# Four graph layers over 50,000 nodes on one core: the bias of the first product's rows moves from VectorE to TensorE, and ScalarE copies the rows out

## The reference

```python
x = _layernorm(x + _L0_gnn_ref(x, edge_index, ...), axis=-1)      # attention, 4 heads, self loops, gelu, layer norm, + x
x = _layernorm(x + _L1_gnn_ref(x, edge_index, ...), axis=-1)      # three GCN hops
x = _layernorm(x + _L2_gnn_ref(x, edge_index, edge_attr_32, ...), axis=-1)   # attention, 8 heads
x = _layernorm(x + _L3_gnn_ref(x, edge_index, edge_attr_64, ...), axis=-1)   # attention, 4 heads
```

```python
h = x @ W_in + b_in
for i in range(Ws.shape[0]):
    xw = h @ Ws[i]
    msg = xw[src] * norm[:, None]
    agg = jax.ops.segment_sum(msg, dst, num_segments=N) + bs[i]
    h = jax.nn.relu(agg)
```

## Time and profile before

| | us |
|---|---|
| median of 3 runs | 4471.79 |
| the runs | 4471.39 to 4476.36 |
| profiled execution, its own time | 4478.09 |
| its span, first to last instruction | 4476.4 |
| VectorE busy | 3477.6 |
| TensorE busy | 2927.3 |
| POOL busy | 2507.9 |
| ScalarE busy | 2496.4 |

### The profile page before, as it was taken

How to read it: one execution, slowest core, us unless ns; L and a number is a source line. 1 busy time by engine, 2 the same in 40 slices (tenths; PEclk the granted TensorE clock), 3 DMA queues, 4 the chain that set the end, 5 groups by cost and what they waited for, 6 DMA issues and landing times. The chain is left out here.

```text
span 4476.4 us, 48774 instructions
## 1 busy us (share of the span) xinstructions
PE 2927.3 (65%) x12128; PEld 1958.3 (44%) x12128; DVE 3477.6 (78%) x8069; ACT 2496.4 (56%) x5486; POOL 2507.9 (56%) x2300
## 2 busy tenths in 40 slices
PE   5776777777761366665554545558888887577775
PEld 3544445444440133333454544435555555344443
DVE  5999999999997766664665659957777776688886
ACT  3777777777774255553332324445656665455554
POOL 6655655555530376201776767768666661566664
PEclk9889888898885677775877765567777777665665
DMA  5776655555552666651444446622222221333331
GB/s 116 182 186 185 191 181 192 188 182 185 189 170 103 182 182 184 185 177 65 150 152 129 149 144 196 194 74 72 63 70 62 69 63 31 99 84 89 92 92 53
DMA packets 383765, 599.12 MB, mean 134 GB/s; under 512 B 124231, under 2 KB 205296, under 8 KB 383486
## 3 DMA queue, kind: packets, MB, share of 16 engines
q1 hardware_dynamic: 313726, 482.99, 35.1%
q0 software_dynamic: 69760, 113.02, 10.2%
HBM read 312.45 MB, written 287.17 MB: 134 GB/s over the span
## 5 line engine op out<-in xcount | busy, mean ns | idle before, releaser
L1551 POOL DMA_INDIRECT gs_g<-table_xw,slot_idx x588 | 594.2, 1010 | 476.4 <-issue 442.1
L900 POOL DMA_INDIRECT gs_t<-table_x,slot_idx x392 | 418.3, 1067 | 306.1 <-issue 204.4
L495 POOL DMA_INDIRECT gs<-x,src_idx x200 | 224.8, 1124 | 437.3 <-DMA xd_rows<-gd 365.1
L368 PE MATMUL ps<-ident,gs_g 128*128 128x128 f32 x588 | 134.8, 372 | 371.9 <-DMA gs_g<-table_xw,slot_idx 371.9
L1589 ACT ACTIVATE hT_g<-u_g 128x512 f32<-128x512 f32 x147 | 92.5, 629 | 498.3 <-DVE u_g L1638 498.3
L1272 POOL DMA_INDIRECT slot_idx<-node_map,src_idx x200 | 230.5, 1153 | 165.8 <-DMA slot_idx<-node_map,src_idx 69.1
L1631 DVE TENSOR_TENSOR_SCAN agg_g<-same_seg,agg_g,ps 128x512 f32<-128x512 uint8 x147 | 188.0, 1279 | 171.7 <-PE ps L368 171.3
L483 POOL DMA_INDIRECT node_map<-slot_no,end_idx x200 | 280.2, 1401 | 61.0 <-issue 60.0
L1785 POOL DMA_INDIRECT out<-x_t,end_idx x196 | 205.7, 1049 | 169.6 <-ACT x_t L339 116.9
L368 PEld LDWEIGHTS ps<-ident,gs_g 128*128 128x128 f32 x588 | 88.3, 187 | 411.2 <-issue 361.3
L495 POOL DMA_INDIRECT gd<-x,dst_idx x200 | 215.8, 1079 | 60.9 <-issue 60.3
(11 more groups left out here) (362 smaller groups left out, 10069.7 us busy)
## 6 DMA issues: line engine op xcount, KB each, us to landing
table_xw<-xw_b SPq DMA_DIRECT2D x147, 512.0 KB, 4.2
table_x<-x_b SPq DMA_DIRECT2D x98, 512.0 KB, 2.8
own_g<-table_xw SPq DMA_DIRECT2D x147, 256.0 KB, 3.7
x_in<-x SPq DMA_DIRECT2D x49, 512.0 KB
out<-hf_b SPq DMA_DIRECT2D x49, 512.0 KB, 2.8
table_xw<-xw_g SPq DMA_DIRECT2D x98, 256.0 KB, 2.3
pen_t<-pen_row SPq DMA_DIRECT2D x98, 256.0 KB, 4.1
xd_rows<-gd SPq DMA_DIRECT2D x50, 256.0 KB, 5.6
```

What stands on the lines that cost most here:

```text
L368: last = nc.tensor.transpose(to[0:width, j * P:(j + 1) * P], t[:, j * width:(j + 1) * width], ident[:])
L495: pool.indirect_dma_start(out=to[k % 3][:, j * D:(j + 1) * D], out_offset=None, in_=x, in_offset=bass.IndirectOffsetOnAxis(ap=of[:, n:n + ...
L900: pool.indirect_dma_start(out=self.B[L % RING][g][:, t * D:(t + 1) * D], out_offset=None, in_=table, in_offset=bass.IndirectOffsetOnAxis(a ...
L1551: pool.indirect_dma_start(out=gs[c % 6][:, j * D:(j + 1) * D], out_offset=None, in_=tables[layer], in_offset=bass.IndirectOffsetOnAxis(ap= ...
```

## The change

The two additions of `xw0_bias` on DVE (L783) are gone. PE puts the bias into the piece of PSUM first, as a product of a row of ones with `xw0_bias4`, a row that holds the bias four times, and adds the four 128x128 products to it. ACT copies the rows out (`xw0_copy`), one half behind each Relu of `h1T`. ACT's wait for `scaled` moves from ahead of the first Relu to ahead of the applies of `x2`.

```diff
--- before.py
+++ after.py
@@ -416,6 +416,7 @@
         rs, nm = ring("rs", 2, (P, 6, 8)), ring("nm", 2, (P, 6, 8))
         big, half_y, hx, wx = (ring(n, 1, (P, 48))[0] for n in ("big", "half_y", "hx", "wx"))
         shifted = tmp.enter_context(nc.sbuf_tensor("shifted", [P, 48], I32))
+        xw0_bias4 = tmp.enter_context(nc.sbuf_tensor("xw0_bias4", [1, CH], F32))
         LNA, LNB, LNC, LND, LNE, LNF = range(6)
         T_XT, T_H, T_G, T_A, T_B, T_C, T_D = ps[:, 0, :], ps[:, 1, :], (ps[:, 2, :], ps[:, 3, :]), ps[:, 4, :], ps[:, 5, :], ps[:, 6, :], ps[:, 7, :]
 
@@ -529,6 +530,14 @@
                     nc.tensor.matmul(T_H[0:8, :], att_src[:], xsT[k % 2][:], start=True, stop=False)
                     nc.tensor.matmul(T_H[0:8, :], att_dst[:], xdT[k % 2][:], start=False, stop=True).then_inc(S("z_ps"), 1)
 
+                def xw0_rows(to, h):
+                    nc.tensor.matmul(to, ones[:], xw0_bias4[:], start=True, stop=False, skip_group_check=True)
+                    for j in range(SUB):
+                        last = nc.tensor.matmul(to[:, j * D:(j + 1) * D], x1T[h][:, j * P:(j + 1) * P], WI0[:],
+                                                start=False, stop=j == SUB - 1, skip_group_check=True)
+                    last.then_inc(S("xw0_ps"), 1)
+
+                pe.wait_ge(S("xw0_bias4"), 1)
                 for t in range(N_CH + 3):
                     f, m = live(t), live(t - 3)
                     c = t - 3
@@ -547,13 +556,13 @@
                         turn(pe, T_B, half(x1_b[c % 3], 1)).then_inc(S("x1T_ps"), 1)
                         pe.wait_ge(S("x1T"), 2 * c + 1)
                         nc.tensor.matmul(T_C, WI0[:], x1T[0][:], start=True, stop=True).then_inc(S("h1_ps"), 1)
-                        rows_times(pe, T_D, x1T[0], WI0).then_inc(S("xw0_ps"), 1)
+                        xw0_rows(T_D, 0)
                     if f:
                         times_W0(t, 0)
                     if m:
                         pe.wait_ge(S("x1T"), 2 * c + 2)
                         nc.tensor.matmul(T_A, WI0[:], x1T[1][:], start=True, stop=True).then_inc(S("h1_ps"), 1)
-                        rows_times(pe, T_B, x1T[1], WI0).then_inc(S("xw0_ps"), 1)
+                        xw0_rows(T_B, 1)
                     if f:
                         turn_x(t, 1)
                     if m:
@@ -597,6 +606,12 @@
                                                     scale=r[:, n, k:k + 1], bias=b[:, n, k:k + 1])
                     last.then_inc(S(ready), 1)
 
+                def xw0_copy(c, h):
+                    act.wait_ge(S("xw0_ps"), 2 * c + h + 1)
+                    if h == 0 and c >= 2:
+                        landed(act, "xw0_out", 2, c - 2)
+                    nc.scalar.copy(half(xw_b[0][c % 2], h), (T_D, T_B)[h]).then_inc(S("xw0"), 1)
+
                 def copy_xT(c, h):
                     act.wait_ge(S("xT_ps"), 2 * c + h + 1)
                     nc.scalar.copy(xT[h][:], T_XT).then_inc(S("xT"), 1)
@@ -622,17 +637,19 @@
                         nc.scalar.copy(x1T[0][:], T_A).then_inc(S("x1T"), 1)
                         act.wait_ge(S("x1T_ps"), 2 * c + 2)
                         nc.scalar.copy(x1T[1][:], T_B).then_inc(S("x1T"), 1)
-                    act.wait_ge(S("scaled"), t + 1)
                     if m:
                         act.wait_ge(S("h1_ps"), 2 * c + 1)
                         nc.scalar.activation(h1T[0][:], T_C, ACT.Relu, bias=h1_bias[:, 0:1]).then_inc(S("h1T"), 1)
+                        xw0_copy(c, 0)
                     if f:
                         gelu(t, 0)
                     if m:
                         act.wait_ge(S("h1_ps"), 2 * c + 2)
                         nc.scalar.activation(h1T[1][:], T_A, ACT.Relu, bias=h1_bias[:, 0:1]).then_inc(S("h1T"), 1)
+                        xw0_copy(c, 1)
                     if f:
                         copy_xT(t, 1)
+                    act.wait_ge(S("scaled"), t + 1)
                     if live(t - 5):
                         q = t - 5
                         if q >= 3:
@@ -705,6 +722,7 @@
                 def blocks(t):
                     return lambda k: t[:, k * D:(k + 1) * D]
 
+                V.tensor_copy(xw0_bias4.rearrange("o (j f) -> o j f", j=SUB), xw0_bias[0:1, None, :].to_broadcast([1, SUB, D])).then_inc(S("xw0_bias4"), 1)
                 for k in range(2):
                     V.memset(raw[k][:], 1.0).then_inc(S("raw"), 1)
                 v.wait_ge(S("raw"), 2)
@@ -774,13 +792,8 @@
                     v.wait_ge(S("batch"), n0 + 10)
                     V.scalar_tensor_tensor(out=b, in0=of[:, :, 1], scalar=-1.0, in1=r, op0=ALU.mult, op1=ALU.mult).then_inc(S("scaled"), 1)
 
-                    m, c, a = live(t - 3), t - 3, t - 1
+                    a = t - 1
                     for h in range(2):
-                        if m:
-                            v.wait_ge(S("xw0_ps"), 2 * c + h + 1)
-                            if h == 0 and c >= 2:
-                                landed(v, "xw0_out", 2, c - 2)
-                            V.tensor_tensor(rows4(half(xw_b[0][c % 2], h)), rows4((T_D, T_B)[h]), each_row(xw0_bias), ALU.add).then_inc(S("xw0"), 1)
                         if live(a):
                             v.wait_ge(S("scaled"), t + 1)
                             v.wait_ge(S("w"), a + 1)
```

## The result

The changed kernel takes 4491.46 us (median of 6 runs, 4487.80 to 4495.41), the kernel before 4471.43 us in its 6 runs (4467.28 to 4476.36): a ratio of 1.0045, 95% interval 1.0032 to 1.0058. It is 20 us slower. The forecast was 4484, 12 us slower, in a range of 4449 to 4497.

A forecast was written before the change was run, and what follows sets the result against it. DVE bound the node stage; the ACT-PE loop would bind next, 26.27 us at full clock, 27.2 with half clock. 40 iterations at +0.23 (+9) and +3 at the ends make +12 us: 4484, range 4449 to 4497.

The forecast's parts named there:

- signs named: Node-stage profile if the loop binds: `nm` wait below 40 us, ACT waiting for PE, DVE for ACT, clock below 0.9.
- bias matmul: PE's one-row, 512-column matmul, two per iteration on the loop: 1.11 us each, bounds 0.86 and 1.97.
- rival B: Node stage: PE's clock stays up, iterations of 26.3 to 26.45 us; 4451 us, wholly at full clock -25 us; chance 0.22.
- half-clock term: Half clock on the loop's PE work adds 0.78 us to 26.27, making 27.05; with recurring stretches, 27.2 was taken.
- the walk: Half-clock stretches 27.3 us apart meet each 26.97 us iteration 0.3 us later, until the iteration comes near 27.3.
- ends of the stage: Node stage's first iterations: two bias matmuls add 2.2 us to each of two, +4, less 1 for those just behind.
- A: The forecast: the loop through PE and ACT binds with half clock on it, +3 to +20 us; chance 0.50 above +9.
- C: No change: clock on the loop stays 0.93, iteration 26.71 us, or a mild loss; medians 4463 to 4481; chance 0.22.
- D: Bias matmuls are hidden and DVE still binds, needing a loop below 25.6 us: -55 us, 4417; chance 0.02.
- E: Worse: more than +20 us, if ACT's late start also makes DVE wait at the hd rows (L800); chance 0.04.

The follow-up runs named there:

- e1: The changed kernel with the two bias matmuls of each iteration left out: 4417.41 us, ratio 0.9873 to the kernel before.
- e6: The changed kernel with the bias row as three bfloat16 parts over 128 rows, added in one pass: 4415.23 us, ratio 0.9870 to the kernel before.
- e4: The changed kernel with three more unused 128x512 matmuls per iteration on PE ahead of the scores: 4463.03 us, ratio 0.9975 to the kernel before.
- e8: Control: the kernel before with three extra unused 128x512 matmuls per iteration ahead of the scores: 4474.18 us, ratio 1.0001 to the kernel before.
- e7: The changed kernel with each bias matmul issued twice in a row: 4643.30 us, ratio 1.0377 to the kernel before.
- e9: The changed kernel with the fp32 bias matmul on operands of 128 rows instead of one: ratio 0.9908 to the kernel before, on a slower chip.
- e3: The changed kernel with ACT's wait for the batch back ahead of the first Relu: 4567.44 us, ratio 1.0209 to the kernel before.
- e5: The changed kernel with the first half's bias matmul issued earlier, ahead of the scores: 4424.35 us, ratio 0.9884 to the kernel before.
- e12: The same kernel as e9 (changed kernel, bias operands of 128 rows), run once more: ratio 0.9886 to the kernel before, on a slower chip.

## Why the prediction was right, and where its sizes were off

**The direction and the mechanism held.** DVE stopped being the bound, the loop through ACT and PE took over (e1 and e6: without the dear matmuls on it DVE binds again), and half clock on that loop turned a gain into a loss (e4: with a clock of 0.97 the same kernel and more work is 28 us faster; e8: not so in the kernel before). Of the signs named, ACT's wait for `nm` fell to nothing, ACT waits 84.2 / 30 = 2.8 us per iteration ahead of the new copies (3 expected), DVE waits 43.1 / 30 = 1.44 us for ACT's rows (1 to 1.6 expected), and the clock over the first 6 us is 0.80 (below 0.9 expected). One sign failed: the iterations do not alternate between 26.3 and 28.

**The bias matmul was mis-sized.** I took 1.11 us. It is 1.25: 1.05 for itself, and 0.10 each for the product ahead of it (L562, 1.06 instead of 0.96; L568 to the second bias 0.96 instead of 0.86) and the rows behind it (0.99 instead of 0.89). The distances in the earlier trace rows had the 1.05; I compared one neighbour and not both. By e7 and e9 this is better read as 0.86 for the matmul and 0.39 for the change between 128 rows and one. Two matmuls, each 0.14 short, are 0.28 us, and the loop at full clock is 26.57, not 26.27. So rival B could at best have brought (26.57 - 26.97) x 40 + 3 = -13 us, not -25.

**The half-clock term was near, its form was not.** I expected a mixture of iterations of 26.3 and 28 that settles at 27.2. The measured mean is 27.31, but there is no mixture: each iteration loses the same 0.73 us. Nor does a first 6 us at 0.80 cost the 1.2 us that I put on it, since part of it is hidden beside ACT's copies. That 27.05 (26.27 + 0.78) came as near as it did owes something to luck: the 0.78 was the mean of a pattern that did not stay. The argument that the stretches recur 27.3 us apart, and that the walk stops when the iteration reaches that, was the part that held best; its number, 27.3, should have been the forecast instead of the 27.2 between two estimates.

**The ends of the stage.** By the starts of the batches, the 37 steady iterations cost 37 x 0.33 = 12.2 us. The four iterations from 74.0 us take 92.0 us instead of 84.5, +7.5, where I had put +4; the next five +0.5 and the three that follow the steady part +2. Together some +22.6, and the last batch starts 23.0 us later (1453.9 against 1430.9). The +3 I had for both ends was +10. The +7.5 belongs to the bias matmuls: without them (e1) the same four iterations take 83.6 us, and the prediction charged only two of them, for two matmuls of 1.1 each.

**Of the rivals,** A held, and with +20 us at the very end of its +3 to +20. C and B needed a clock of 0.93 and 0.95 or more; it was 0.80. D was excluded by the loop. E's wait at the hd rows did not come (DVE's only waits are those at L821); it did come in e3 (41.6 us), where ACT starts its part late, and in e7 (80.9 us), where the loop was made longer.

**One row or 128.** The Trainium skill, "TensorE: Matmul & The Clock Gate", has a matmul of few rows cost as much as one of 128. Counted alone that agrees with this case: a one-row fp32 matmul behind another adds 0.86 us in e7, and one of 128 rows takes 0.86 in e9. But one that stands between products of 128 rows costs 1.25 in all, and that is the case of this kernel. The Trainium skill's advice in the closing table, to leave PE few idle gaps, is borne out by e4, which that advice would have led to, and brings nothing in e8, where PE is not on the loop. For the changed kernel alone I took it to mean 4451 us, and it measured 4491: the change closes one gap (PE goes from the turn of the next columns at 720.29 straight to the second product at 720.73) but not the one ahead of the scores, 2.30 us.

## What to carry to other kernels

Before work is moved off the engine that binds, write down the loop that will bind next, at full and at half TensorE clock: slack that hides PE also hides its clock (e8), and once the slack is used, what half clock costs shows on the loop (0.73 us per iteration here, won back in e4 by filling one idle gap). A product that adds a bias belongs in PE's idle time (e5) or in a cheap form (e6: three bfloat16 parts over 128 rows, 0.22 us instead of 1.25). And where half-clock stretches recur at a distance a little longer than the iteration, ask whether the iteration may be drawn to that distance; one kernel here shows it.

## What was not expected of the hardware

- The iteration settled at 27.31 us and stayed there within 0.04 us for 37 iterations, with PE at half clock for the last 7.8 us of each and the first 2.5 us of the next.
- A 128x512 fp32 matmul with one-row operands between 128-row ones costs 0.39 us more than one of 128 rows at full clock (e4, e9), and the next one-row matmul behind it nothing more (e7): the change costs, not the row.
- Useless matmuls in idle time made a kernel 28 us faster (e4 against the changed kernel).
- Two chips ran the kernel before in 4739 and 4736 us instead of 4471. The node-stage iterations of e9 to e12, which ran there, are disturbed; no trace of the kernel before was taken on them, and what the cause is stays open.
